# One-hot routing tables with the token index innermost, and a prefix over tiles summed by TensorE

## What is computed

```python
logits = x_flat @ router_w.T                      # 2048 tokens x 7 experts
top_vals, top_idx = jax.lax.top_k(logits, TOP_K)  # two picks per token
top_w = jax.nn.softmax(top_vals, axis=-1)
...
routed_out = _swiglu(x_flat, w_gate, w_up, w_down)
mixed = jnp.einsum('end,ne->nd', routed_out, combine)
mixed = mixed + jnp.mean(shared_out, axis=0)
```

## Time and profile before

| | us |
|---|---|
| median of 3 runs | 486.38 (486.29, 486.38, 487.9) |
| the profiled execution | 487.31 |
| its span | 485.5 |
| PE busy in the span | 416.2 (86%) |
| DVE busy | 325.7 (67%) |
| ACT busy | 244.5 (50%) |
| POOL busy | 133.8 (28%) |

### The profile page before, as it was taken

How to read it: one execution, slowest core, us unless ns; L and a number is a source line. 1 busy time by engine, 2 the same in 40 slices (tenths; PEclk the granted TensorE clock), 3 DMA queues, 4 the chain that set the end, 5 groups by cost and what they waited for, 6 DMA issues and landing times. The chain is left out here.

```text
span 485.5 us, 10662 instructions
## 1 busy us (share of the span) xinstructions
PE 416.2 (86%) x3980; PEld 255.0 (53%) x3980; DVE 325.7 (67%) x823; ACT 244.5 (50%) x416; POOL 133.8 (28%) x220
## 2 busy tenths in 40 slices
PE   1869899999999999999989878897999999999500
PEld 0533433435243433435244364655699999999500
DVE  5899978797988888797963936499433333333277
ACT  1531167776777677686776707653233233233240
POOL 8200000100111110100110013334667766763332
PEclk9985589999999999999998959999999999999955
DMA  7554750303021020000000017100577687877152
GB/s 218 198 180 142 244 160 20 90 2 88 3 63 28 11 81 2 2 2 4 1 3 3 0 53 208 44 2 0 169 216 248 209 253 247 238 221 239 43 161 86
DMA packets 46694, 50.77 MB, mean 105 GB/s; under 512 B 5363, under 2 KB 34420, under 8 KB 46644
## 3 DMA queue, kind: packets, MB, share of 16 engines
q1 hardware_dynamic: 43632, 44.77, 30.1%
q0 software_dynamic: 2432, 4.99, 3.6%
q10 hardware_dynamic: 580, 0.33, 0.3%
HBM read 36.90 MB, written 12.98 MB: 103 GB/s over the span
## 5 line engine op out<-in xcount | busy, mean ns | idle before, releaser
L640 ACT ACTIVATE probs<-banks 128x1024 f32<-128x1024 f32 (+1 forms) x192 | 145.3, 810 | 59.1 <-PE banks L495 48.0
L786 DVE TENSOR_REDUCE mx_part<-banks 128x1 f32<-128x512 f32 (+2 forms) x224 | 130.2, 646 | 15.9 <-PE banks L476 7.5
L470 PE MATMUL banks<-k_st,q_st 64*128 64x512 bf16 (+3 forms) x384 | 115.7, 354 | 8.0 <-DVE parts L754 4.2
L488 PE MATMUL banks<-q_st,k_st 64*128 64x512 bf16 (+3 forms) x384 | 97.5, 333 | 6.2 <-ACT probs L640 5.9
L507 PE MATMUL banks<-probs,v_pad 128*32 128x512 f32 (+3 forms) x768 | 83.3, 506 | 0.0
L1525 DVE TENSOR_TENSOR hidden<-banks,gate 128x512 f32<-128x512 f32 x38 | 26.3, 692 | 66.2 <-PE banks L1192 66.2
L488 PEld LDWEIGHTS banks<-q_st,k_st 64*128 64x128 bf16 x384 | 31.1, 95 | 60.9 <-ACT probs L640 49.0
L786 DVE TENSOR_REDUCE mx<-banks 128x1 f32<-128x512 f32 (+3 forms) x96 | 51.9, 596 | 16.5 <-PE banks L476 15.2
L470 PEld LDWEIGHTS banks<-k_st,q_st 64*128 64x128 bf16 x384 | 34.4, 95 | 36.3 <-DVE mx_part L786 27.7
L474 PE MATMUL banks<-mask_qk,ident_half 64*128 64x128 bf16 x256 | 52.6, 231 | 0.0
L493 PE MATMUL banks<-mask_kq,ident_half 64*128 64x128 bf16 x256 | 49.3, 221 | 0.0
(11 more groups left out here) (199 smaller groups left out, 572.2 us busy)
## 6 DMA issues: line engine op xcount, KB each, us to landing
w_g<-in_w_gate SPq DMA_DIRECT2D x38, 256.0 KB
w_u<-in_w_up SPq DMA_DIRECT2D x38, 256.0 KB
q_st<-q_rows SPq DMA_DIRECT2D x32, 128.0 KB, 2.9
k_st<-k_rows SPq DMA_DIRECT2D x32, 128.0 KB, 2.9
w_d<-in_w_down SPq DMA_DIRECT2D x8, 256.0 KB, 5.1
back<-results SPq DMA_DIRECT2D x8, 256.0 KB, 4.7
q_rows<-parts SPq DMA_DIRECT2D x4, 384.0 KB, 3.0
k_rows<-parts SPq DMA_DIRECT2D x4, 384.0 KB, 3.5
```

The lines of the kernel that those rows point to most:

```text
L470: last = nc.tensor.matmul(dst[:, at:at + width], q_st[r][rows, c, p, (i % CH) * P:(i % CH + 1) * P], k_st[r][rows, kc, p, 0:width], start= ...
L488: last = nc.tensor.matmul(dst[a][:, 0:width], k_st[r][rows, j // CH, p, (j % CH) * P:(j % CH + 1) * P], q_st[r][rows, c, p, first:BANK], s ...
L640: nc.scalar.activation(probs[unit % PROBS][:, 2 * p:2 * p + 2, first:BANK], slot_pair[k % 2].rearrange("p (a t) -> p a t", a=2)[:, :, 0:BA ...
L786: nc.vector.tensor_reduce(dst, taken[:, :, 0:width], AX.X, ALU.max, negate=True).then_inc(max_taken, 1)
```

## The change

The tables `row_hot` and `tile_hot` are stored with the token tile innermost (row_hot[p, pick, row, tile], tile_hot[p, pick, value, tile slot, tile]); the operands that they are compared with become bf16 (`slot_part_f`, `iota_ct`, and a new constant `iota_rep` of 128 x 128 x 16 that repeats each number 16 times, made by POOL). PE therefore reads a column of either table with a step of 16 elements, 32 bytes. The addition over tiles moves from DVE to PE: 15 more products with the square of ones, with shifts 1 to 15, go into `rank_bank`, which moves to another PSUM bank; `total_bank` is computed first and has a release of its own. DVE sums it by one reduction (`sums`). The slots of both picks are multiplied and reduced in one instruction each. The cut diff:

```diff
-        iota_ct = sb("iota_ct", [P, 2 * NT])
+        iota_ct = sb("iota_ct", [P, 2 * NT], BF16)
+        iota_rep = sb("iota_rep", [P, P, NT], BF16)
...
-        slot_part_f = sb("slot_part_f", [P, 2, 2 * NT])
-        row_hot = sb("row_hot", [P, 2 * NT, P], BF16)
-        tile_hot = sb("tile_hot", [P, 2 * NT, 3, TILES], BF16)
+        slot_part_f = sb("slot_part_f", [P, 2, 2 * NT], BF16)
+        row_hot = sb("row_hot", [P, 2, P, NT], BF16)
+        tile_hot = sb("tile_hot", [P, 2, 3, TILES, NT], BF16)
...
-            rank_bank = t_bank[:, 2 * P + 3 * TILES:2 * P + 3 * TILES + E * NT]
+            rank_bank = xt_bank[0][:, 0:E * NT]
...
+                                                 (iota_rep[:, :, :], [[1, P], [0, NT]], 0, 0),
...
                 flat = picked[:, :, :].rearrange("p e t -> p (e t)")
-                nc.tensor.matmul(rank_bank, upper[:, :], flat, start=True, stop=True).then_inc(counted, 1)
                 nc.tensor.matmul(total_bank, ones_b[:, :], flat, start=True, stop=True).then_inc(counted, 1)
+                nc.tensor.matmul(rank_bank, upper[:, :], flat, start=True, stop=False)
+                rank = rank_bank.rearrange("p (e t) -> p e t", e=E)
+                for shift in range(1, NT):
+                    last = nc.tensor.matmul(rank[:, :, shift:], ones_b[:, :], picked[:, :, 0:NT - shift],
+                                            start=False, stop=(shift == NT - 1))
+                last.then_inc(counted, 1)
...
-                    last = nc.tensor.matmul(t_out, row_hot[:, k, :],
-                                            tile_hot[:, k, :, :].rearrange("p v a -> p (v a)"),
+                    last = nc.tensor.matmul(t_out, row_hot[:, k // NT, :, k % NT],
+                                            tile_hot[:, k // NT, :, :, k % NT].rearrange("p v a -> p (v a)"),
...
-                dve.wait_ge(counted, 2)
-                nc.vector.tensor_copy(before[0][:, :, KT:], total_bank.rearrange("p (e t) -> p e t", e=E)
-                                      ).then_inc(steps, step.one())
-                for i, shift in enumerate((1, 2, 4, 8)):
-                    src, dst = before[i % 2], before[(i + 1) % 2]
-                    done()
-                    nc.vector.tensor_tensor(dst[:, :, KT:], src[:, :, KT:], src[:, :, KT - shift:KT + NT - shift],
-                                            ALU.add).then_inc(steps, step.one())
-                done()
-                sums = before[0]
-
-                nc.vector.tensor_tensor(over[:, :, :], sums[:, :, KT + NT - 1:KT + NT].broadcast_to([P, E, NT]),
+                dve.wait_ge(counted, 1)
+                nc.vector.tensor_reduce(sums[:, :, 0], total_bank.rearrange("p (e t) -> p e t", e=E), AX.X, ALU.add
+                                        ).then_inc(steps, step.one())
+                done()
+
+                nc.vector.tensor_tensor(over[:, :, :], sums[:, :, :].broadcast_to([P, E, NT]),
                                         thresholds[:, :].unsqueeze(1).broadcast_to([P, E, NT]), ALU.is_gt
                                         ).then_inc(steps, step.one())
-                nc.vector.tensor_tensor(slot_in[:, :, :], rank_bank.rearrange("p (e t) -> p e t", e=E),
-                                        sums[:, :, KT - 1:KT + NT - 1], ALU.add).then_inc(steps, step.one())
...
+                dve.wait_ge(counted, 2)
                 nc.vector.scalar_tensor_tensor(slot_all[:, :, :], end[:, 3:3 + E].unsqueeze(2).broadcast_to([P, E, NT]),
-                                               float(P), slot_in[:, :, :], ALU.mult, ALU.add
+                                               float(P), rank_bank.rearrange("p (e t) -> p e t", e=E),
+                                               ALU.mult, ALU.add
                                                ).then_inc(steps, step.one())
                 done()
-                for i in range(2):
-                    nc.vector.tensor_tensor(slot_pick[i][:, :, :], slot_all[:, :, :], pick[i][:, :, :], ALU.mult
-                                            ).then_inc(steps, step.one())
-                done()
-                for i in range(2):
-                    nc.vector.tensor_reduce(slot_f[:, i, :], slot_pick[i][:, :, :].rearrange("p e t -> p t e"),
-                                            AX.X, ALU.add).then_inc(steps, step.one())
+                nc.vector.tensor_tensor(slot_pick[:, :, :, :], slot_all[:, :, :].unsqueeze(1).broadcast_to([P, 2, E, NT]),
+                                        pick_all[:, :, :, :], ALU.mult).then_inc(steps, step.one())
+                done()
+                nc.vector.tensor_reduce(slot_f[:, :, :], slot_pick[:, :, :, :].rearrange("p i e t -> p i t e"),
+                                        AX.X, ALU.add).then_inc(steps, step.one())
...
                 for i in range(2):
                     part = slice(i * NT, (i + 1) * NT)
                     nc.vector.tensor_tensor(
-                        tile_hot[:, part, 2, :], iota[:, 0:TILES].unsqueeze(1).broadcast_to([P, NT, TILES]),
-                        slot_part_f[:, 0, part].unsqueeze(2).broadcast_to([P, NT, TILES]), ALU.is_equal
+                        tile_hot[:, i, 2, :, :], iota_rep[:, 0:TILES, :],
+                        slot_part_f[:, 0, part].unsqueeze(1).broadcast_to([P, TILES, NT]), ALU.is_equal
+                    ).then_inc(steps, step.one())
+                    nc.vector.tensor_tensor(
+                        row_hot[:, i, :, :], iota_rep[:, :, :],
+                        slot_part_f[:, 1, part].unsqueeze(1).broadcast_to([P, P, NT]), ALU.is_equal
                     ).then_inc(steps, step.one())
                     done()
-                    nc.vector.tensor_scalar(tile_hot[:, part, 0, :], tile_hot[:, part, 2, :], iota_p[:, 0:1],
+                    nc.vector.tensor_scalar(tile_hot[:, i, 0, :, :], tile_hot[:, i, 2, :, :], iota_p[:, 0:1],
                                             None, ALU.mult).then_inc(steps, step.one())
                     nc.vector.tensor_tensor(
-                        tile_hot[:, part, 1, :], tile_hot[:, part, 2, :],
-                        iota_ct[:, part].unsqueeze(2).broadcast_to([P, NT, TILES]), ALU.mult
-                    ).then_inc(steps, step.one())
-                    nc.vector.tensor_tensor(
-                        row_hot[:, part, :], iota[:, :].unsqueeze(1).broadcast_to([P, NT, P]),
-                        slot_part_f[:, 1, part].unsqueeze(2).broadcast_to([P, NT, P]), ALU.is_equal
+                        tile_hot[:, i, 1, :, :], tile_hot[:, i, 2, :, :],
+                        iota_ct[:, part].unsqueeze(1).broadcast_to([P, TILES, NT]), ALU.mult
                     ).then_inc(steps, step.one())
```

More of the change, by code:

```diff
@@ L882, in program @@
         gap_sum = sb("gap_sum", [P, NT])
-        pick = [sb(f"pick{i}", [P, E, NT]) for i in range(2)]
+        pick_all = sb("pick_all", [P, 2, E, NT])
+        pick = [pick_all[:, i, :, :] for i in range(2)]
         picked = sb("picked", [P, E, NT], BF16)
-        before = [sb(f"before{i}", [P, E, KT + NT]) for i in range(2)]
+        sums = sb("sums", [P, E, 1])
         over = sb("over", [P, E, NT])
         ends = [sb(f"ends{i}", [P, 4 + E]) for i in range(2)]
-        slot_in = sb("slot_in", [P, E, NT])
         slot_all = sb("slot_all", [P, E, NT])
-        slot_pick = [sb(f"slot_pick{i}", [P, E, NT]) for i in range(2)]
+        slot_pick = sb("slot_pick", [P, 2, E, NT])
         slot_f = sb("slot_f", [P, 2, NT])
@@ L1034, in _ @@
                 nc.gpsimd.memset(ones_b[:, :], 1.0).then_inc(route_consts, 1)
-                pool.wait_ge(route_consts, 7)
+                pool.wait_ge(route_consts, 8)
                 nc.gpsimd.affine_select(out=upper[:, :], in_=zeros2[:, :], compare_op=ALU.is_ge, fill=1.0,
@@ L1156, in _ @@
                 pe.wait_ge(picked_ready, 1)
-                pe.wait_ge(route_consts, 8)
+                pe.wait_ge(route_consts, 9)
                 flat = picked[:, :, :].rearrange("p e t -> p (e t)")
-                nc.tensor.matmul(rank_bank, upper[:, :], flat, start=True, stop=True).then_inc(counted, 1)
                 nc.tensor.matmul(total_bank, ones_b[:, :], flat, start=True, stop=True).then_inc(counted, 1)
+                nc.tensor.matmul(rank_bank, upper[:, :], flat, start=True, stop=False)
[4 more added lines that the diff above has]
+                last.then_inc(counted, 1)
                 shared_down(1)
@@ L1326, in _ @@
                 nc.vector.memset(logits[:, :, E:8], NEG).then_inc(steps, step.one())
-                for buf in before + ends:
+                for buf in ends:
                     nc.vector.memset(buf[:], 0.0).then_inc(steps, step.one())
@@ L1377, in _ @@
                 done()
-                dve.wait_ge(route_consts, 8)
+                dve.wait_ge(route_consts, 9)
                 for i in range(2):
```

## The result

The changed kernel takes 491.64 us (median of 4 runs, 491.32 to 492.62) against 486.34 us: 1.0104 times as long, with a 95% interval of 1.0083 to 1.0125. It is slower by 5.3 us. The forecast was 488.0 us with a range of 485.0 to 490.8; the time lies above the range. The profiled execution took 492.62 us with a span of 490.9.

The account below looks back on a forecast made before the run. The prediction took the chain of waits through PE, ACT and POOL as the bound. +0.78 (products) -1.5 (POOL) +2.3 (step) = +1.6 us on the median 486.38 gave 488.0 us, range 485.0 to 490.8.

Parts of the forecast that it names:

- The step: PE's 32 table products: reading columns 32 bytes apart costs 73 ns more a pair, +2.3 us.
- rival 2: Table products: the step is dear, 1.61 ns an element, 206 ns a pair; +4.2 us, 490.6 us; chance 0.17.
- Which side: Table products: the step's extra was priced on 128 elements a pair, 128 x 0.57 = 73 ns.
- POOL: POOL's three products on the path: 4.2 us instead of 5.70 as DVE's table work leaves room, -1.5 us.
- The 15 products: PE's added products before shared_down(1), fully on the path at 52 ns each: +0.78 us.
- DVE's part: DVE's routing work: cast to slot_part_f ends at 324.6, both tables at 329.6; the gain itself worth nothing.
- Rival 3: DVE's tables: 16-bit comparisons run no faster, tables last until 333 and hold up POOL; +4.0, 490.4 us; chance 0.08.
- rival 1: Table products: the step costs PE nothing; -0.7, 485.7 us, at best 484.9; chance 0.27.

Follow-up runs that it names:

- rows_step: The changed kernel with tile_hot stored side by side as before, so only row_hot is read with a step of 32 bytes; 486.05 us, one run.
- step4: The changed kernel with 4 instead of 16 token tiles innermost, both tables read with a step of 8 bytes; 486.92 us (1.0011).
- long_dense: rows_step with its 32 table products done three more times into another PSUM bank that nobody reads; 491.55 us, one run.

## Why the prediction was wrong

- **The step** is the term that failed: +5.14 us against the +2.3 that I took. I had two readings of the same pair of rows, an extra of 0.57 ns an element (+2.3) and a floor of 1.61 ns an element (+4.9, rival 2), and chose the smaller as the one "which carries over what the row shows and no more". The runs show a floor: 1.81 to 1.86 ns per 16-byte piece, at either clock. PE takes 52 / 114 = 0.46 ns a column without a step, so its extra is about 1.4 ns, not DVE's 0.57. That DVE's 1.61 lies near 1.85 may be luck: no run gives DVE's time for a new piece, and the two rows behind the 0.57 differ in the number of outputs too (16 and 7).
- **Which side** pays was also wrong in the working: I multiplied by the 128 columns of the weights. It is the 114 of the moving side; the stepped weights cost 10 ns a pair. Rival 2's 206 ns came near the measured 212 by way of the wrong side; on 114 columns its 1.61 ns would have given 184 ns, +4.2 us. The Trainium skill's rule on the fast weight load (TensorE: Matmul & The Clock Gate, section Weight-path perf modes) is that it takes packed and strided columns alike. rows_step does not speak against that, with 62 ns a pair against 52; whether the fast load was at work no run shows. The Trainium skill's rule on lines of 16 bytes (Advanced Engine Details and Errata, section SBUF Cachelines) is that accesses slow down when each goes to a new line, and that two hits on a line are needed. It holds for the moving side but for the number of hits: with two (8 bytes) the products took 3.38 us, twice what they took with four (1.72).
- **The clock** was in no term and in no rival: +1.48 us in the last piece of the path (+1.64 in the four slow products of `shared_up`, 0.16 less behind them). With the other measured terms alone, +0.46 - 1.63 + 5.14, the outcome would have been 490.4 us, within the range; the clock took it beyond the end. The profile of before had a granted clock of 1.00 in this whole stretch, and lower means elsewhere (0.84 in the first 50 us). The upper end of the range was made of durations at a clock that I took as given.
- **POOL** was right in mechanism and size: three products in 4.07 us against 4.2 forecast, -1.63 against -1.5. The 0.3 us charged for L1467 (here L1466) came another way than told: POOL's first product was ahead of it, and the second lost 0.27 us beside it.
- **The 15 products**: +0.46 against +0.78. 0.46 / 15 = 31 ns each; so a full square of weights need not cost 52 ns, and the columns (0.38) set most of it.
- **DVE's part** came out as worked: `over` waited for POOL's product (840 ns against 0.28 + 0.51 = 0.79), the cast to `slot_part_f` ended at 324.28, on the clock of the earlier trace rows 324.7, forecast 324.6; the two tables 4.9 us against 5.0. Rival 3 is out. `hot_ready` was earlier for PE than the working says: its own figures, 329.6 for the tables and 333.9 + 3.84 = 337.7 for PE, are eight microseconds apart, not four (329.2 and 336.9 in the run). Nothing hung on it.
- **The range** was said to run from rival 1's best to rival 2's sum; these are 484.9 and 490.6, not 485.0 and 490.8. The outcome is beyond either.
- **The sum** with the measured terms, +0.46 - 1.63 + 5.14 + 1.48 = +5.45, is the measured 5.3 within 0.2 us. That the change doesn't reach outside its stretch was right: the expert loop ran at its pace, and at a clock of 1.00.

## What to carry to other kernels

An operand that TensorE streams is better laid out with at least four 16-bit columns in every 16 bytes: a step of 4 bytes was free here and VectorE still made its table in 1.22 instead of 2.28 us, while 8 bytes doubled the products and 16 bytes or more took four times as long. The weights may be stepped (62 against 52 ns a pair), so of two tables the one that must have a step belongs on that side. When a layout change helps one engine, price what it does to the reader of the table as the reader's own floor per access, not as another engine's extra; and when work comes off a neighbour, look whether that lets something on the path move into a wait.

## What the runs showed that I had not expected

- On the moving side each new 16-byte piece took 1.81 to 1.86 ns in four kernels, nearly the same at a granted clock of 1.00 and 0.50 (a pair every 211 and 214 ns in the change).
- In every kernel with table products at 207 to 212 ns a pair the granted clock went from 1.00 to 0.50 in them or right behind, and the f32 products that followed took twice their time (3.42 instead of 1.72 us for four in the change). The same products at 106 ns a pair (step4) and at 62 (rows_step, and long_dense with four times as many) left it at 1.00.
- POOL's new constant of 2048 elements took 2.48 us, not the 1.8 forecast from smaller ones; it ended at 290.7 and nothing waited for it.
